# Causal mask of 128 tokens' scores: one 128-column matmul, or three rows of contraction and four triangles of 32

## The chip, the cores and the metric

The kernel runs on one core of a Trainium2 chip. The metric is the device time of one execution in microseconds. Engines: TensorE (PE: matmuls; PEld: its weight loads), VectorE (DVE), ScalarE (ACT), GpSimd (POOL) and SyncE (SP), which here only issues DMAs.

## The reference

Sixteen sequences of 256 tokens, 128 features wide, go through a mixture of experts, an attention with forget gates, and the same mixture again. What matters here is the attention:

```python
scores = jnp.einsum('bhid,bhjd->bhij', q, k) * scale       # 16 heads of 8
scores = scores + c[..., :, None] - c[..., None, :]         # c: cumulated log of the forget gates
causal = jnp.tril(jnp.ones((n, n), dtype=bool))
scores = jnp.where(causal, scores, NEG)                     # NEG = -1e30
attn = jax.nn.softmax(scores, axis=-1)
out = jnp.einsum('bhij,bhjd->bhid', attn, v)
```

## The kernel before

**Stages.** run_layers gives each engine its order of work: steps of the first mixture, then the attention, then the second mixture, with a few steps of two stages woven together at the borders. The attention goes through the 16 sequences as a pipeline; step s of it has six parts (j = 0 to 5), and in each part an engine does its share of sequence s (direct scores and their maxima), of s-1 (turned scores, exponentials, products with v), of s-2 (output projection) and of s+1, s+2 (projections to come). The steps in the middle are a loop of three unrolled steps (run_steps); the first two and the last three are written out. All engines run through their own list and meet at semaphores.

**Direct scores** (scores, called twice in each part, p = 0 to 11). They serve only for the row maxima of the softmax; the first starts at 111.2 us, the last mask at 364.3. For p = 0 to 3 (the first 128 tokens, t == 0) one matmul L881 takes four heads at once: q_dense (stationary, 104 rows of contraction) against k_heads (512 columns), into one of two PSUM banks. The 104 rows hold a split of q and k in three parts and the gates' sums, for four groups of heads; k_heads is zero outside a head's own group. For p = 4 to 11 (tokens 128 to 255) L886 does two heads in two matmuls of 256 columns. Then the mask: L889 adds ident16 (bfloat16, 128 x 128) times mask16 to the diagonal blocks of the bank, 4 x 128 columns for p < 4, 2 x 128 otherwise, and raises scores_ready. VectorE's row_max (L794) takes the negated maximum of the bank and raises max_done; scores p waits for the maximum of p-2, since the bank is the same.

**Turned scores** (L901, 12 a sequence, n = 0 to 11) are the transposed scores with the maxima as further rows of contraction, 512 columns each. The rows above the 106th are another form of the same mask: three rows later_q (-1e30 for queries ahead of token 32, 64, 96) against later_k (one for keys in the 32 tokens from there on) mask whole blocks of 32; what is left above the diagonal inside the blocks is cleared by GpSimd (L673) after the exponential. ScalarE takes the exponential of each (L733); L901 number n waits for exponential n-2. In part 0 ScalarE also copies turned maxima (L720, from the transpose L930) and issues two DMAs that put them into q_rows (L725), between exponentials 0 and 1.

**Products with v** (times_v, L916): for each of six pairs of exponentials, eight products of 32 stationary columns and 128 moving ones, each of which stands in the trace as two records (32 records in two calls). Their outputs go to partitions 32g to 32g+32 of a bank, g = 0 to 3 in turn.

**Order on TensorE in part 0**: scores 0, scores 1, turn_max (L930), L901 twice. **Part 1**: scores 2, scores 3, the projection of v (L960), L901 twice, L916 32 times.

**DMAs.** SP loads q_dense and k_heads for the next sequence from DRAM staging (L600, L603) once scores 3 of the current one are done (scores_ready). They fill rows 0 to 95 of q_dense (96 to 103 stay 1.0 from set_up_dense) and all 104 of k_heads. At the start constant_rows (L569) waits for the fills on GpSimd (dense_set, later_set) and sends constant rows to q_rows and k_rows by DMA (the issue of the last of them ends at 43.9 us); TensorE waits for all of them (ones_in, L940) ahead of the first score.

Of the kernel before, what the change touches and what calls it, by code (L numbers as in the profile page):

```python
# [5 lines left out]
FP32R = mybir.dt.float32r  # L6
# [6 lines left out]
P = 128  # L13
# [4 lines left out]
def at_least(eng, sem, value):  # L18

    if isinstance(value, int) and value <= 0:  # L20
        return
    eng.wait_ge(sem, value)
# [443 lines left out]
def attention_layer(nc, ctx, c, made, banks, x_all, S_LEN, before):  # L466
# [13 lines left out]
    H, D = c["H"], P  # L480
    NSEQ = x_all.shape[1] // 2
    HD = D // H
    NG, NU = 4, H // 4
    HW = 16
    ROWS = 3 * HD + 2
    KR = NG * ROWS
    KM = KR + 2
    KD = KM + 3
    SCALE = float(HD) ** -0.5
    N = S_LEN  # L490
    sb = lambda name, shape, dt: ctx.enter_context(nc.sbuf_tensor("a_" + name, shape, dt))
# [20 lines left out]
    k_parts = sb("k_parts", [P, 2, N], FP32R)  # L512
    q_rows = [sb(f"q_rows{b}", [KD, H, N], FP32R) for b in range(3)]
    k_rows = [sb(f"k_rows{b}", [KD, NU, N], FP32R) for b in range(3)]
    q_dense = sb("q_dense", [KR, NU, P], FP32R)
    k_heads = sb("k_heads", [KR, H, P], FP32R)
    v_sb = [sb(f"v{b}", [P, 2 * H // 2, 3, HW], FP32) for b in range(3)]
    neg_max = sb("neg_max", [P, 2, H], FP32)
    max_parts = sb("max_parts", [P, 2, 2, H], FP32R)
# [6 lines left out]
    ident16 = sb("ident16", [P, P], BF16)  # L526
    mask16 = sb("mask16", [P, 4, P], BF16)
    later_q = sb("later_q", [3, 2, P], FP32)
    later_k = sb("later_k", [3, 2, P], FP32)
# [8 lines left out]
    set_up, zeroed, ones_in, v_zeroed = sem("set_up"), sem("zeroed"), sem("ones_in"), sem("v_zeroed")  # L538
# [9 lines left out]
    scores_ready, max_done = sem("scores_ready"), sem("max_done")  # L548
# [12 lines left out]
    raw = lambda tile: tile[(slice(None),) * len(tile.shape)].bitcast(FP32)  # L561
# [7 lines left out]
    def constant_rows(sp):  # L569
        sp.wait_ge(zeroed, 4)  # L570
        ones = ones_r[:, :].bitcast(FP32).rearrange("r (u n) -> r u n", u=NU)
        for b in range(3):
            for g in range(NG):
                sp.dma_start(raw(q_rows[b])[NG * 3 * HD + g:KR:NG, NU * g:NU * (g + 1), :], ones).then_inc(ones_in, 16)
            sp.dma_start(raw(k_rows[b])[KR:KM, :, :], ones).then_inc(ones_in, 16)
        sp.wait_ge(dense_set, 2)
        sp.wait_ge(later_set, 5)
        for b in range(3):
            sp.dma_start(raw(q_rows[b])[KM:KD, :, :], later_q[:, :, :].rearrange("a t n -> a (t n)").unsqueeze(1)
                         .broadcast_to([3, H, N])).then_inc(ones_in, 16)  # L580
            sp.dma_start(raw(k_rows[b])[KM:KD, :, :], later_k[:, :, :].rearrange("a t n -> a (t n)").unsqueeze(1)
                         .broadcast_to([3, NU, N])).then_inc(ones_in, 16)
# [40 lines left out]
    def zero_rows(act, b):  # L623

        act.wait_ge(zero_set, 1)
        nc.scalar.activation(q_rows[b][:, :, :], zero_row[0:KD, :].unsqueeze(1).broadcast_to([KD, H, N]),
                             ACT.Copy).then_inc(zeroed, 1)
# [88 lines left out]
    def scalar(act):  # L716
# [23 lines left out]
        def part(i, s, j):  # L740
# [15 lines left out]
            if j == f_part(s) + 2 and F:  # L756
                act.wait_ge(qk_ready, n)
                at_least(act, q_stored, (n - 1) * 16 * 3)
                at_least(act, k_stored, (n - 1) * 16 * 3)
                nc.scalar.activation(q_parts[:, 0, :], q_ps, ACT.Copy, scale=SCALE)  # L760
                nc.scalar.activation(k_parts[:, 0, :], k_ps, ACT.Copy).then_inc(qk_hi_done, 1)
# [25 lines left out]
    def vector(dve):  # L787
# [39 lines left out]
        def part(i, s, j):  # L827
# [24 lines left out]
            if j == f_part(s) + 2 and F:  # L852
                dve.wait_ge(qk_hi_done, n)
                nc.vector.scalar_tensor_tensor(out=q_parts[:, 1, :], in0=q_ps, scalar=SCALE,
                                               in1=q_parts[:, 0, :].bitcast(FP32), op0=ALU.mult, op1=ALU.subtract).then_inc(qk_lo_done, 1)
# [18 lines left out]
    def tensor(pe):  # L874
        def scores(i, s, p):
            at_least(pe, max_done, i * 12 + p - 1)
            b, bank = s % 3, score_bank[p % 2]
            t, heads = (0, 4) if p < 4 else (1, 2)
            keys = (t + 1) * P
            if t == 0:  # L880
                nc.tensor.matmul(bank[:, :], q_dense[:, p, :], k_heads[:, p:H:NU, :], start=True, stop=False,  # L881
                                 skip_group_check=True)
            else:
                for n in range(heads):
                    h = 2 * (p - 4) + n
                    nc.tensor.matmul(bank[:, n * keys:(n + 1) * keys], q_rows[b][0:KR, h, P:N],  # L886
                                     k_rows[b][0:KR, h % NU, :], start=n == 0, stop=False, skip_group_check=True)
            own = bank[:, :].rearrange("p (h n) -> p h n", h=heads)[:, :, keys - P:keys]
            nc.tensor.matmul(own, ident16[:, :], mask16[:, 0:heads, :], start=False, stop=True,  # L889
                             skip_group_check=True).then_inc(scores_ready, 1)  # L890

        def turned_scores(i, s, n):
            if n == 0:
# [5 lines left out]
            t, u, jt = (0, n, 0) if n < 4 else (1, (n - 4) // 2, n % 2)  # L899
            rows = KD if jt == t else KM  # L900
            nc.tensor.matmul(bank[:, :], k_rows[b][0:rows, u, jt * P:(jt + 1) * P],  # L901
# [31 lines left out]
        def part(i, s, j):  # L933
# [3 lines left out]
                pe.wait_ge(w_ordered, 2)  # L937
            if s == 0 and j == 0:
                pe.wait_ge(set_up, 2)
                pe.wait_ge(ones_in, 16 * 3 * (NG + 3))  # L940
                pe.wait_ge(before["tiles_done"], 2 * NSEQ)
                pe.wait_ge(before["high_used"], 2 * NSEQ)

# [3 lines left out]
            if S:  # L947
                scores(i, s, 2 * j)
                scores(i, s, 2 * j + 1)
# [4 lines left out]
            if j == 1 and V:  # L954
# [4 lines left out]
                for t in range(2):  # L959
                    last = nc.tensor.matmul(side_bank[:, t * D:(t + 1) * D], xt[:, t * P:(t + 1) * P], c["Wv"][:, :],  # L960
                                            start=True, stop=True)
                last.then_inc(v_ready, 1)
            if j == 2 and F:
                at_least(pe, qk_lo_done, (n - 1) * 2)
                pe.wait_ge(xn_done, n)
                for t in range(2):
                    last = nc.tensor.transpose(proj_bank[:, t * P:(t + 1) * P], xn[:, t], c["ident"][:, :])
# [14 lines left out]
            if j == 4 and T:  # L982
# [7 lines left out]
                for t in range(2):  # L990
                    last = nc.tensor.transpose(side_bank[:, t * P:(t + 1) * P],
                                               attn[:, t].rearrange("p h d -> p (h d)"), c["ident"][:, :])
                last.then_inc(attn_t_ready, 1)
            if j == 5 and T:
                pe.wait_ge(attn_t_copied, i - 1)
                for t in range(2):
                    last = nc.tensor.matmul(side_bank[:, t * D:(t + 1) * D], attn_t[:, t * P:(t + 1) * P], c["Wo"][:, :],  # L997
                                            start=True, stop=True)
# [22 lines left out]
def program(nc, x, Wq, Wk, Wv, Wo, Wf, Wg, We, be, out):  # L1021
# [5 lines left out]
    with ExitStack() as ctx:  # L1027
# [17 lines left out]
        tiles = moe_tiles(nc, ctx, E, Q, D)  # L1045
        moe1 = moe_layer(nc, ctx, c, made, tiles, banks, x_all, "m1_", x_dram=x_rows)
        attention = attention_layer(nc, ctx, c, made, banks, x_all, N, before=moe1)
        moe2 = moe_layer(nc, ctx, c, made, tiles, banks[1:5] + [banks[0], banks[7]], x_all, "m2_",
                         out_dram=out_rows, before=attention)
# [72 lines left out]
```

## Time and profile before

| | us |
|---|---|
| runs, median of 3 | 467.35 (465.76 to 472.85) |
| the profiled execution's own time | 468.03 |
| its span, from first to last instruction | 465.9 |
| TensorE busy | 404.1 (87%) |
| VectorE busy | 362.4 (78%) |
| ScalarE busy | 278.5 (60%) |
| GpSimd busy | 249.7 (54%) |
| mean granted clock of TensorE | 0.978 |

All rows come from one profiled execution. Times of day are us from the start of its span. A record of a matmul begins when the instruction begins, which may be before its weights are loaded, and its end is modelled; so lengths are compared with each other and starts give the pace. "idle before <- X" tells how long the engine did nothing ahead of an instruction and who released it; "issue" means that no wait is seen. Some matmul records are missing.

### The profile page before, as it was taken

The page shows a single profiled execution, that of the slowest core. Times are in us where ns is not written, and L with a number is a line of the kernel's source. Part 1 is how long each engine was busy: PE and PEld are TensorE (multiplying, and loading weights), DVE is VectorE, ACT ScalarE, POOL GpSimd, SP SyncE. Part 2 cuts the span into 40 slices and gives each one's busy share as a digit, 9 for nine tenths or more (in the row PEclk, how much of TensorE's full clock was granted, in tenths as well). Part 3 has the DMA queues.
Part 4 walks back from the last instruction along what each step waited for, and adds up shares of the span by engine and source line. Part 5 has one row for each costly group of instructions (what it writes and reads, how often), then busy time and mean ns, then how long its engine had stood idle before and what let it go on. Part 6 is the DMA issues. An engine that isn't in the chain of part 4 may idle for free.

```text
span 465.9 us, 11688 instructions
## 1 busy us (share of the span) xinstructions
PE 404.1 (87%) x3280; PEld 287.6 (62%) x3296; DVE 362.4 (78%) x1284; ACT 278.5 (60%) x758; POOL 249.7 (54%) x431
## 2 busy tenths in 40 slices
PE   0778888775799999999999999999998898888884
PEld 0656666553466666666667666766765676666652
DVE  3989999986877786686677678677666458999995
ACT  4666777352275566657566566655656567667753
POOL 8976666543245544544554454454445435676654
PEclk9999999887999999999999999999999899999998
DMA  3311000035644354344535535443540000001001
GB/s 112 92 56 22 0 1 0 1 100 148 171 118 152 117 155 116 111 139 111 149 102 147 134 102 149 113 147 108 152 130 9 6 1 1 25 24 45 23 23 45
DMA packets 45792, 39.11 MB, mean 84 GB/s; under 512 B 5896, under 2 KB 42524, under 8 KB 45754
## 3 DMA queue, kind: packets, MB, share of 16 engines
q1 hardware_dynamic: 43706, 38.14, 29.0%
q10 hardware_dynamic: 2048, 0.53, 0.6%
q8 instruction: 17, 0.28, 0.3%
q14 instruction: 21, 0.17, 0.1%
HBM read 22.61 MB, written 15.20 MB: 81 GB/s over the span
## 4 chain that ended last, share of the span: by engine, by line
PE 43%; POOL 22%; issue 14%; ACT 8%; DVE 5%; DMA 2%; ACTq 2%; SPq 2%; POOLq 1%; DVEq 0%
PE bank L916 10%; POOL m_pair L217 9%; PE bank L901 8%; PE bank L886 6%; ACT a_weights L733 5%; POOL m_upper L221 4%; PE bank L889 4%; PE bank L881 4%; POOL m_rstd L229 3%; PE bank L997 2%; PE bank L1008 2%; ACTq L725 2%; PE bank L1011 2%; DVE a_neg_max L794 1%; DMA x_all<-in_L_attn_x 1%
## 5 line engine op out<-in xcount | busy, mean ns | idle before, releaser
L794 DVE TENSOR_REDUCE a_neg_max<-bank 128x2 f32<-128x512 f32 (+1 forms) x192 | 123.7, 685 | 62.6 <-PE bank L889 59.9
L673 POOL TENSOR_SCALAR_AFFINE_SELECT a_weights<-a_weights 128x512 f32<-128x512 f32 (+1 forms) x96 | 75.5, 787 | 108.7 <-ACT a_weights L733 104.0
L733 ACT ACTIVATE a_weights<-bank 128x512 f32<-128x512 f32 x192 | 107.0, 591 | 35.0 <-issue 22.0
L251 ACT ACTIVATE m_scaled<-bank,m_gates 128x128 f32<-128x128 f32 x256 | 72.3, 365 | 26.2 <-PE bank L417 26.2
L901 PE MATMUL bank<-a_q_rows,a_k_rows 106*128 106x512 f32 (+1 forms) x192 | 73.7, 451 | 4.9 <-ACT a_weights L733 4.9
L217 POOL TENSOR_TENSOR m_pair<-m_scaled 128x256 f32<-128x256 f32 x64 | 47.5, 742 | 50.8 <-ACT m_scaled L251 50.7
L294 DVE SCALAR_TENSOR_TENSOR m_lower<-bank,m_gates,m_lower 128x128 f32<-128x128 f32 x192 | 66.0, 344 | 2.3 <-issue 0.2
L886 PE MATMUL bank<-a_k_rows,a_q_rows 104*128 104x256 f32 x256 | 59.3, 335 | 0.4 <-DVE a_neg_max L794 0.4
L889 PE MATMUL bank<-a_mask,a_ident 128*128 128x256 bf16 (+1 forms) x176 | 56.2, 320 | 0.0
L916 PE MATMUL bank<-a_weights,a_v 128*32 128x128 f32 x1536 | 52.7, 279 | 0.0
L886 PEld LDWEIGHTS bank<-a_k_rows,a_q_rows 104*128 104x128 f32 x256 | 40.6, 194 | 14.5 <-DVE a_neg_max L794 10.1
L916 PEld LDWEIGHTS bank<-a_weights,a_v 128*32 128x32 f32 x1536 | 39.6, 111 | 8.9 <-issue 6.4
L416 PE MATMUL bank<-we_hi,m_xt_hi 128*128 128x512 f32 x64 | 32.1, 502 | 11.9 <-DVE m_lower L294 11.3
L901 PEld LDWEIGHTS bank<-a_q_rows,a_k_rows 106*128 106x128 f32 (+1 forms) x192 | 30.9, 193 | 13.4 <-ACT a_weights L733 11.4
L881 PE MATMUL bank<-a_k_heads,a_q_dense 104*128 104x512 f32 x64 | 31.1, 524 | 5.9 <-DMA a_k_heads<-k_stage 4.4
L720 ACT ACTIVATE a_max_t<-bank 32x128 fp32r<-32x128 f32 x32 | 8.5, 265 | 42.3 <-PE bank L930 42.3
L221 POOL TENSOR_TENSOR m_upper<-m_pair 128x128 f32<-128x128 f32 x64 | 29.6, 463 | 5.7 <-POOL m_pair L217 1.3
L889 PEld LDWEIGHTS bank<-a_mask,a_ident 128*128 128x128 bf16 x192 | 19.0, 99 | 19.4 <-issue 12.5
L275 ACT ACTIVATE m_xn<-x_all,m_shift,m_rstd 128x128 f32<-128x128 f32 (+1 forms) x64 | 26.3, 484 | 4.6 <-POOL m_shift L233 4.5
L416 PEld LDWEIGHTS bank<-we_hi,m_xt_hi 128*128 128x128 f32 x64 | 12.5, 196 | 22.6 <-DVE m_lower L294 22.1
L417 PE MATMUL bank<-we_hi,m_xt_hi 128*128 128x512 f32 x64 | 26.2, 409 | 0.0
L417 PE MATMUL bank<-we_lo,m_xt_hi 128*128 128x512 f32 x64 | 26.2, 409 | 0.0
(128 smaller groups left out, 828.5 us busy)
## 6 DMA issues: line engine op xcount, KB each, us to landing
a_k_rows<-k_stage SPq DMA_DIRECT2D x16, 416.0 KB
k_stage<-a_k_parts SPq DMA_DIRECT2D x48, 128.0 KB, 1.8
q_stage<-a_q_parts SPq DMA_DIRECT2D x48, 128.0 KB, 1.9
a_q_rows<-q_stage SPq DMA_DIRECT2D x64, 96.0 KB
a_k_heads<-k_stage SPq DMA_DIRECT2D x64, 52.0 KB
a_q_dense<-q_stage SPq DMA_DIRECT2D x16, 192.0 KB
x_all<-in_L_attn_x SPq DMA_DIRECT2D x8, 256.0 KB, 2.8
out_x<-x_all SPq DMA_DIRECT2D x8, 256.0 KB, 2.3
```

Of the source, the lines that this page charges most:

```text
L217: nc.gpsimd.tensor_tensor(pair[:, q % 2], scaled[:, q % 2, 0:2], scaled[:, q % 2, 2:4], ALU.add).then_inc(pair_done, 1)
L251: last = nc.scalar.activation(scaled[:, q % 2, j], y_high[q % 2][:, j * D:(j + 1) * D], ACT.Copy, scale=gates[:, s % 2, q, 4 + j:5 + j])
L294: nc.vector.scalar_tensor_tensor(out=lower[:, q % 2, j], in0=y_low[q % 2][:, j * D:(j + 1) * D], scalar=gates[:, s % 2, q, j:j + 1], in1=t ...
L417: last = nc.tensor.matmul(y_high[q % 2][:, :], x_part, w_part[:, H:2 * H], start=k == 0, stop=k == 2)
L673: nc.gpsimd.affine_select(out=diagonal, in_=diagonal, compare_op=ALU.is_ge, fill=0.0, base=0, pattern=[[0, heads.stop - heads.start], [1, P]],
L733: nc.scalar.activation(weights[n // 2][:, half:half + 4, :].rearrange("p h n -> p (h n)"), wt_bank[n % 2][:, :], ACT.Exp).then_inc(wt_exp, 1)
L794: nc.vector.tensor_reduce(neg_max[:, t, heads], score_bank[p % 2][:, :].rearrange("p (h n) -> p h n", n=(t + 1) * P), AX.X, ALU.max, negat ...
L881: nc.tensor.matmul(bank[:, :], q_dense[:, p, :], k_heads[:, p:H:NU, :], start=True, stop=False, skip_group_check=True)
L886: nc.tensor.matmul(bank[:, n * keys:(n + 1) * keys], q_rows[b][0:KR, h, P:N], k_rows[b][0:KR, h % NU, :], start=n == 0, stop=False, skip_g ...
L889: nc.tensor.matmul(own, ident16[:, :], mask16[:, 0:heads, :], start=False, stop=True, skip_group_check=True).then_inc(scores_ready, 1)
L901: nc.tensor.matmul(bank[:, :], k_rows[b][0:rows, u, jt * P:(jt + 1) * P], q_rows[b][0:rows, u:H:NU, t * P:(t + 1) * P], start=True, stop=T ...
L916: last = nc.tensor.matmul(out_bank[t][32 * g:32 * (g + 1), u // 2 * P:(u // 2 + 1) * P], v_sb[b][:, jt * H // 2 + 2 * g + u // 2, u % 2:u ...
```

## The change

For p < 4 the mask of whole blocks goes into L881 as three more rows of contraction (later_q and later_k, as L901 has them, set once at the start by two more DMAs), and only the triangles inside the four diagonal blocks of 32 are added by matmuls: four, one for each block of 32 queries, each with 32 stationary columns of ident16 and 4 x 32 moving columns of mask16, into 32 partitions. For p > 3 nothing changes.

```diff
--- before.py
+++ after.py
@@ -486,6 +486,7 @@
     KR = NG * ROWS
     KM = KR + 2
     KD = KM + 3
+    KL = KR + 3
     SCALE = float(HD) ** -0.5
     N = S_LEN
     sb = lambda name, shape, dt: ctx.enter_context(nc.sbuf_tensor("a_" + name, shape, dt))
@@ -512,8 +513,8 @@
     k_parts = sb("k_parts", [P, 2, N], FP32R)
     q_rows = [sb(f"q_rows{b}", [KD, H, N], FP32R) for b in range(3)]
     k_rows = [sb(f"k_rows{b}", [KD, NU, N], FP32R) for b in range(3)]
-    q_dense = sb("q_dense", [KR, NU, P], FP32R)
-    k_heads = sb("k_heads", [KR, H, P], FP32R)
+    q_dense = sb("q_dense", [KL, NU, P], FP32R)
+    k_heads = sb("k_heads", [KL, H, P], FP32R)
     v_sb = [sb(f"v{b}", [P, 2 * H // 2, 3, HW], FP32) for b in range(3)]
     neg_max = sb("neg_max", [P, 2, H], FP32)
     max_parts = sb("max_parts", [P, 2, 2, H], FP32R)
@@ -575,6 +576,8 @@
             sp.dma_start(raw(k_rows[b])[KR:KM, :, :], ones).then_inc(ones_in, 16)
         sp.wait_ge(dense_set, 2)
         sp.wait_ge(later_set, 5)
+        sp.dma_start(raw(q_dense)[KR:KL, :, :], later_q[:, 0:1, :].broadcast_to([3, NU, P])).then_inc(ones_in, 16)
+        sp.dma_start(raw(k_heads)[KR:KL, :, :], later_k[:, 0:1, :].broadcast_to([3, H, P])).then_inc(ones_in, 16)
         for b in range(3):
             sp.dma_start(raw(q_rows[b])[KM:KD, :, :], later_q[:, :, :].rearrange("a t n -> a (t n)").unsqueeze(1)
                          .broadcast_to([3, H, N])).then_inc(ones_in, 16)
@@ -886,8 +889,15 @@
                     nc.tensor.matmul(bank[:, n * keys:(n + 1) * keys], q_rows[b][0:KR, h, P:N],
                                      k_rows[b][0:KR, h % NU, :], start=n == 0, stop=False, skip_group_check=True)
             own = bank[:, :].rearrange("p (h n) -> p h n", h=heads)[:, :, keys - P:keys]
-            nc.tensor.matmul(own, ident16[:, :], mask16[:, 0:heads, :], start=False, stop=True,
-                             skip_group_check=True).then_inc(scores_ready, 1)
+            if t == 0:
+                for g in range(4):
+                    block = slice(32 * g, 32 * (g + 1))
+                    last = nc.tensor.matmul(own[block, :, block], ident16[:, block], mask16[:, 0:heads, block],
+                                            start=False, stop=True, skip_group_check=True)
+            else:
+                last = nc.tensor.matmul(own, ident16[:, :], mask16[:, 0:heads, :], start=False, stop=True,
+                                        skip_group_check=True)
+            last.then_inc(scores_ready, 1)
 
         def turned_scores(i, s, n):
             if n == 0:
@@ -937,7 +947,7 @@
                 pe.wait_ge(w_ordered, 2)
             if s == 0 and j == 0:
                 pe.wait_ge(set_up, 2)
-                pe.wait_ge(ones_in, 16 * 3 * (NG + 3))
+                pe.wait_ge(ones_in, 16 * (3 * (NG + 3) + 2))
                 pe.wait_ge(before["tiles_done"], 2 * NSEQ)
                 pe.wait_ge(before["high_used"], 2 * NSEQ)
 
```

## Rows read from the trace of the kernel before

**Rows 1.** The page: busy time by engine; the chain that ended last.

```profile
PE 404.1 (87%) x3280; PEld 287.6 (62%) x3296; DVE 362.4 (78%) x1284; ACT 278.5 (60%) x758; POOL 249.7 (54%) x431
...
PE 43%; POOL 22%; issue 14%; ACT 8%; DVE 5%; DMA 2%; ACTq 2%; SPq 2%; POOLq 1%; DVEq 0%
PE bank L916 10%; POOL m_pair L217 9%; PE bank L901 8%; PE bank L886 6%; ACT a_weights L733 5%; POOL m_upper L221 4%; PE bank L889 4%; PE bank L881 4%; POOL m_rstd L229 3%; PE bank L997 2%; PE bank L1008 2%; ACTq L725 2%; PE bank L1011 2%; DVE a_neg_max L794 1%; DMA x_all<-in_L_attn_x 1%
```

**Rows 2.** Stretches: us, busy us of PE, PEld, DVE, ACT, POOL, clock, DMA share.

```profile
108.00:156.88 48.88, 41.40 (x331) 27.56 (x334) 36.82 (x86) 23.03 (x56) 19.58 (x34) 0.93 0.48 137
223.08:239.52 16.44, 15.81 (x165) 11.07 (x165) 12.17 (x30) 10.19 (x24) 7.98 (x14) 1.00 0.47 127
288.92:304.99 16.07, 15.72 (x165) 11.02 (x165) 12.08 (x30) 10.07 (x24) 7.90 (x14) 1.00 0.48 130
```

**Rows 3.** Groups by shape of TensorE: count, busy us, mean ns of one.

```profile
L916 PE MATMUL bank<-a_weights,a_v 128*32 128x128 f32 x1536 | 52.7, 279 | 0.0
L889 PE MATMUL bank<-a_mask,a_ident 128*128 128x256 bf16 x128 | 36.7, 286 | 0.0
...
L889 PE MATMUL bank<-a_mask,a_ident 128*128 128x512 bf16 x48 | 19.6, 408 | 0.0
```

**Rows 4.** The chain through one loop sequence: start us, us, what.

```profile
224.84 0.56 ACT a_weights L733
225.43 0.61 ACTq L725
...
226.15 0.61 ACT a_weights L733
...
226.80 0.50 PE bank L901
```

**Rows 5.** Timeline of TensorE, same sequence: start us, us, operation.

```profile
223.40 0.59 PE L881 MATMUL bank<-a_k_heads,a_q_dense 104*128 104x512 f32 x1
223.83 0.39 PE L889 MATMUL bank<-a_mask,a_ident 128*128 128x512 bf16 x1
...
224.06 0.27 PE L930 MATMUL bank<-ident,a_max_parts 128*32 128x128 f32 x1
...
224.79 0.40 PE L881 MATMUL bank<-a_k_heads,a_q_dense 104*128 104x512 f32 x1
...
225.13 0.53 PE L881 MATMUL bank<-a_k_heads,a_q_dense 104*128 104x512 f32 x1
...
225.73 0.61 PE L960 MATMUL bank<-wv,a_xt 128*128 128x128 f32 x4
226.10 0.48 PE L901 MATMUL bank<-a_q_rows,a_k_rows 109*128 109x512 f32 x1
226.80 0.50 PE L901 MATMUL bank<-a_q_rows,a_k_rows 109*128 109x512 f32 x1 [0.22 <-ACT a_weights L733]
```

**Rows 6.** Into and out of L916, matmuls (PE) and weight loads (PEld).

```profile
222.68 0.40 PE L916 MATMUL bank<-a_weights,a_v 128*32 128x128 f32 x8
...
223.01 0.19 PEld L881 LDWEIGHTS bank<-a_k_heads,a_q_dense 104*128 104x128 f32 x1 [0.20 <-issue]
223.01 0.51 PE L881 MATMUL bank<-a_k_heads,a_q_dense 104*128 104x512 f32 x1
...
227.23 0.32 PE L916 MATMUL bank<-a_weights,a_v 128*32 128x128 f32 x4
...
228.24 0.30 PEld L886 LDWEIGHTS bank<-a_k_rows,a_q_rows 104*128 104x128 f32 x2 [0.20 <-issue]
```

**Rows 7.** The two L901 behind L960, in a sequence behind the loop.

```profile
307.97 0.96 PE L901 MATMUL bank<-a_q_rows,a_k_rows 109*128 109x512 f32 x2
```

**Rows 8.** First sequence: the weight load of p=2 and what it waited for.

```profile
113.21 0.29 PEld L881 LDWEIGHTS bank<-a_k_heads,a_q_dense 104*128 104x128 f32 x1 [0.41 <-DVE a_neg_max L794]
```

**Rows 9.** SP's queue at the end of the set-up and its next work.

```profile
41.28 1.83 SPq L579 DMA_DIRECT2D a_q_rows<-a_later_q  x1
...
96.58 1.32 SPq L609 DMA_DIRECT2D k_stage<-a_k_parts  x3
```

## The prediction

> **What bounds the kernel now.** I read the page's busy shares and its chain first [rows 1]: TensorE is busy for 87% of the span and carries 43% of the chain; the mask line L889 alone has 4% of the chain and L881, the product ahead of it, another 4%. Next the busy time in stretches [rows 2]. One sequence of the attention takes 16.44 us in the middle of the loop, and TensorE is busy for 15.81 us of it at a granted clock of 1.00; near the end a sequence takes 16.07 us. So the attention, from 111 to 364 us, is bound by TensorE, and time taken from or given to it there should show, unless another engine's wait lies over it. The groups by shape [rows 3] give the operation that is replaced: the 512-column mask lasts 408 ns by its record, against 286 ns for the 256-column one of the second half. The difference, 0.12 us for 256 columns, is what columns cost at the full clock: 0.06 us for 128. (The view has 48 records of the 64 wide masks that the loops give; some are missing.)
>
> The chain of one sequence [rows 4] then says which wait ends last. After the first turned score (L901), the chain goes to ScalarE: an exponential, the issue of a DMA (L725, 0.61 us), a second exponential, and back to L901 at 226.80. In that stretch TensorE isn't the bound, so what is done behind the first L901 and ahead of the one at 226.80 has cover. Scores p=0 and p=1 of a sequence stand ahead of that chain, p=2 and p=3 stand beside it.
>
> **How TensorE's time is read from its records** [rows 5]. A record of 512 columns lasts 0.39 to 0.40 us when its weight load was hidden; what is above that at its front is its load. So L881 for p=1 (starts 223.40, lasts 0.59) streams from 223.60; the one of p=0 streams from 223.13 (record 223.01, 0.12 of load ahead). Streams of p=0 and p=1 are 0.47 us apart; from p=1's to L930 (224.06) it is 0.46. For p=2 the stream begins at 224.80, p=3's at 225.27 (225.13 and 0.14), L960 at 225.73: 0.47 and 0.46 again. Of each 0.47, 0.23 is L881 and 0.24 is L889.
>
> **What the change adds in each of the four scores.** It takes out one load of 128 columns and one matmul of 512 columns and puts in four loads of 32 columns and four matmuls of 128 columns, whose outputs stand in four groups of 32 partitions. This form is in the kernel already: L916 has 32 stationary columns and 128 moving ones, and its outputs also go round the four groups. Its records in [rows 6]: two quads of four begin 0.11 us apart (eight records in flight last 0.40, one lasts 0.28), so the four groups do stream side by side. But it pays at both ends. Entering: the L901 ahead of it (226.80, 0.50 long, so 0.11 of load) has streamed by 227.12 to 227.14, and the first load of L916 starts at 227.23, though nothing else is late: 0.10 us of nothing. Its own first load stands in front, 0.02, and the four start 0.02 apart in all (four records take 0.32 against 0.30 for one). Leaving: the last quad streams until about 222.91, and the load of L881 starts at 223.01, 0.20 after the loader's last work: again 0.10 us of nothing, and then the 0.11 us of that load is in the open, where it is otherwise hidden under the matmul before. Between plain matmuls no such gap is seen: L889's record for p=1 starts at 223.83, where L881's 0.23 are over. L930, a transpose with 32 columns, starts right behind L889's 0.23 (224.06), so the width alone doesn't bring the gap; I take it that a transpose stays in the plain form.
>
> The Trainium skill, TensorEngine Tiling (Array Packing), Key Properties, says that a change of tiling mode, not of the tile alone, drains the engine; it has no figure. By that rule the new masks pay at both ends as L916 does, and the trace's 0.10 us is its price. The same page's Theoretical Speedup promises up to 4x for a dimension of 32 or less; by that alone the mask would go from 0.24 to about 0.06 us, which is the first rival below.
>
> So one score after the change, from L881's stream to the next stream: 0.23 (L881) + 0.10 (enter) + 0.02 (load) + 0.02 (four starts) + 0.06 (128 columns) + 0.10 (leave) + 0.11 (next load in the open) = 0.64.
> - p=0: 0.64 for 0.47, +0.17.
> - p=1: L930 follows, whose 32-column load costs some 0.03 in the open in place of 0.11: 0.56 for 0.46, +0.10.
> - p=2: +0.17. p=3: L960 follows, with a full load: 0.64 for 0.46, +0.18.
> The bounds of the unknown, that is of what bfloat16 quads behind a float32 product do: below, no gap at all (0.33, so -0.14 each); above, both gaps at L916's price. I take the upper one, as L916's rows are the nearest in form. Going below it would need the gap to belong to what L916 reads, and its gap on leaving is the same ahead of L881 and, at 228.24, ahead of L886 [rows 6].
>
> **What of it lies on the path.** p=0 and p=1 delay L901, and the ScalarE chain with it: +0.27 a sequence. p=2 and p=3 are +0.35 more, but TensorE waits for ScalarE afterwards: the L901 at 226.10 streams from 226.19 and is through at 226.42, the next one streams only from 226.91. That is 0.49 us of cover in a loop sequence, so the 0.35 is hidden; without this cover it would cost 0.35 x 15 = 5.3 us. In the three sequences behind the loop the two L901 last 0.96 together [rows 7], so the second streams from 308.54 where it could from 308.29: cover 0.25, and 0.10 us comes through. The first sequence has no turned scores beside it and runs at a lower clock; its p=2 waits 0.41 us for VectorE's maximum [rows 8], which partly covers a longer mask. Between 0 and 0.8 us, I take 0.4.
> Later stations of a sequence (row maxima, exponentials, the causal selects on GpSimd) follow TensorE and move with it. VectorE gets a mask's result no later for p=0: the last quarter starts about 0.37 us after L881's stream and lasts some 0.23 (L889's 0.286 less 0.06 for 128 columns), together 0.60, against 0.24 + 0.39 = 0.63 now. The three further rows of contraction in L881 cost nothing: L901 with 109 rows has the same record length, 0.50, as L881 with 104, 0.51 [rows 5, 6].
> Sum: 15 x 0.27 = 4.05; 3 x 0.10 = 0.30; 0.4; together 4.75 us.
>
> **Set-up.** Two more DMAs stand in SP's queue ahead of the six of L579 and L581, of which the longest issue takes 1.83 us [rows 9]. So up to 3.7 us, and the last would be issued by 47.6 in place of 43.9; SP has nothing more until 96.58. The cover is some 49 us; without it the attention would start 3.7 us later. TensorE's wait at the first score asks for two more DMAs on the same semaphore, which have landed long before 111 us. The two fills on GpSimd get three more partitions and no more elements in each.
>
> **The sum against the time.** The profiled execution took 468.03 us (span 465.9 and 2.1 around it), so it would become 472.8. It was 0.68 above the median of the runs, 467.35; the forecast for the median is 472.1.
>
> **Rivals.**
> - *The quads stream beside everything without a gap.* Then p=0 takes 0.23 + 0.02 + 0.02 + 0.06 = 0.33 for 0.47, the same for p=1 unless the issue of L930 and L901 holds them back; p=2 and p=3 only lengthen the wait for ScalarE. 15 x 0.14 to 15 x 0.28 is 2.1 to 4.2 us less: 465.2 to 463.1. It decides where a gap plus open load costs less than 0.14 together. For it: the quads of L916 do overlap. Against: the gaps around L916, at each of its groups that I looked at. Chance 0.12. The skill's page TensorE: Matmul & The Clock Gate, Measured speedup vs the span model, has a pack of tiles last one matmul and some 4 ns a tile, which says the same of the inside and nothing of the ends.
> - *The cover over p=2 and p=3 is gone,* because ScalarE's DMA issue or exponentials come sooner and TensorE is again the last. Then 0.62 x 15 + 0.4 = 9.7 us: 477.1. For it: the sequences behind the loop have only half the cover. Against: 0.61 us of DMA issue stands in every loop sequence. Chance 0.10.
> - *Nothing shows,* because the longer masks fall into waits for VectorE's maxima, as in rows 8, or the gap is smaller next to a bfloat16 quad: 467 to 469. For it: the L881 of p=3 already has 0.14 us of its load in the open (0.53 for 0.39) [rows 5]. Chance 0.12.
> - *The clock.* Eight more gaps in a sequence lower TensorE's activity, and the granted clock, 1.00 in the middle [rows 2], falls in stretches. The attention's first 48.88 us had 0.93; a mean of 0.93 is 14% of the time at half speed (1.2 GHz in place of 2.4), which loses up to 7% of 250 us, 17 us, and with half of it under other waits still 8 us over the forecast: 480 and up. Chance 0.04.
>
> **The numbers.** Forecast 0.62, with its own range of 469.5 to 474.5: 472.1 us. For 8 in 10 the range reaches to where the first and second rival begin: 465.0 to 477.1. A change of 2% (9.3 us) is about what a measurement can tell: faster than 458.0 lies beyond the first rival's end, 0.01; slower than 476.7 is most of the second and the fourth, 0.10; within, 0.89.
>
> **What the profile after would show.** Right: a gap of about 0.10 us ahead of the first 32-column mask load and behind the last quarter, L881 records of about 0.50 (load in the open) for p=1 and p=3; streams of p=0 and p=1 0.64 apart; the idle time of the L901 at the ScalarE wait shorter by some 0.35; the sequence in the loop at about 16.7 us in place of 16.44. Wrong: the L881 of p=1 starting 0.33 behind p=0's (first rival), or a sequence of 17.1 us with no wait for ScalarE left (second), or granted clocks under 1.00 between 130 and 350 us (fourth).

## The result and the profile after

The change made the kernel slower: 474.78 us median of 4 runs (473.20 to 476.32) against 467.29 for the kernel before (465.76 to 472.85), a ratio of 1.0157 with a 95% interval of 1.0109 to 1.0205. That is 7.5 us by the medians, where 4.75 were forecast. (The ratios here and below are those of the record, which aren't the quotients of the medians; for some of the kernels the two differ by 0.4%.) The profiled execution took 476.32 us, its span is 474.3.

The page of the kernel after: busy time, granted clock in 40 slices of 11.9 us, and the chain. They answer to [rows 1].

```profile
PE 413.4 (87%) x3488; PEld 292.6 (62%) x3488; DVE 362.8 (76%) x1284; ACT 278.5 (59%) x758; POOL 249.5 (53%) x431
...
PEclk9999999995579999899999999999999979999999
...
PE 47%; POOL 21%; issue 14%; ACT 6%; DVE 5%; DMA 2%; SPq 2%; ACTq 1%; POOLq 1%; DVEq 0%
```

The mean granted clock fell from 0.978 to 0.960; slices 10 and 11 show 5 tenths, and slice 12 shows 7, where the first two sequences of the attention run. In the trace the clock is low (0.50) from 108.4 to 135.7 us. The busy time in stretches (us, busy us of PE, PEld, DVE, ACT, POOL, clock, DMA share), first after, answering to [rows 2]: the first two sequences, one with a dip of the clock, one in the loop, one behind it.

```profile
109.72:126.60 16.88, 14.83 (x57) 9.15 (x58) 10.84 (x24) 2.85 (x9) 2.67 (x5) 0.50 0.45 122
126.60:144.01 17.41, 17.38 (x136) 11.52 (x137) 11.45 (x26) 9.53 (x22) 7.42 (x12) 0.74 0.45 125
193.76:212.34 18.58, 17.52 (x181) 11.98 (x177) 12.98 (x32) 10.13 (x24) 8.73 (x15) 0.91 0.44 125
245.31:261.81 16.50, 16.07 (x181) 11.12 (x177) 12.08 (x30) 10.12 (x24) 7.98 (x13) 1.00 0.44 126
294.78:311.06 16.28, 15.93 (x181) 11.10 (x177) 12.04 (x30) 10.06 (x24) 7.90 (x13) 1.00 0.44 128
```

The first two of before, cut at the same places, that is from one sequence's first score to the next:

```profile
111.18:125.27 14.09, 11.34 (x44) 7.21 (x46) 10.72 (x24) 2.65 (x8) 2.67 (x5) 0.77 0.53 147
125.27:139.96 14.69, 13.71 (x124) 9.21 (x125) 11.24 (x26) 9.38 (x22) 7.41 (x12) 1.00 0.53 148
```

Here is the time. The first two sequences take 34.29 us in place of 28.78, +5.51, at a clock of 0.50 and 0.74 for 0.77 and 1.00. The one with the dip takes 18.58 against 16.61 for its counterpart, +1.97; the clock was low there for 3.4 us. The other loop sequences don't get longer: the first of them takes 16.75 for 16.86, the seven others have a mean of 16.49 us, and the eight of before one of 16.51. The three sequences behind the loop take 16.28, 16.25 and 16.24 for 16.07, 16.08 and 16.64, and the one after them, up to the last sequence's first score, 14.62 for 14.02. The rest of the span's 8.4 us is a start of the attention 1.46 us earlier and an end (from the last sequence's first score on) 1.88 us longer, both in stages that the change doesn't touch. The clock was at its lower level there too: ahead of the attention for twice 3.4 us in the profile of before and not at all in this one, and in the second mixture for 3.4 us before and 6.8 us after.

The groups by shape, answering to [rows 3]:

```profile
L884 PE MATMUL bank<-a_k_heads,a_q_dense 107*128 107x512 f32 x64 | 32.9, 514 | 5.3 <-DMA a_k_heads<-k_stage 4.1 <-DVE a_neg_max L797 1.0 <-issue 0.2
...
L895 PE MATMUL bank<-a_mask,a_ident 128*32 128x128 bf16 x256 | 15.8, 238 | 0.0
```

And TensorE in a loop sequence, with VectorE's addition L874 (L871 of before) beside it, answering to [rows 5, 6]:

```profile
244.97 0.40 PE L926 MATMUL bank<-a_weights,a_v 128*32 128x128 f32 x8
...
245.30 0.19 PEld L884 LDWEIGHTS bank<-a_k_heads,a_q_dense 107*128 107x128 f32 x1 [0.20 <-issue]
...
245.67 0.41 DVE L874 TENSOR_TENSOR x_all<-x_all,bank 128x256 f32 x1
245.72 0.10 PEld L895 LDWEIGHTS bank<-a_mask,a_ident 128*32 128x32 bf16 x4 [0.24 <-issue]
245.73 0.24 PE L895 MATMUL bank<-a_mask,a_ident 128*32 128x128 bf16 x4
...
245.89 0.19 PEld L884 LDWEIGHTS bank<-a_k_heads,a_q_dense 107*128 107x128 f32 x1
...
246.32 0.24 PE L895 MATMUL bank<-a_mask,a_ident 128*32 128x128 bf16 x4
246.49 0.10 PEld L940 LDWEIGHTS bank<-ident,a_max_parts 128*32 128x32 f32 x1
...
246.53 0.30 PEld L911 LDWEIGHTS bank<-a_q_rows,a_k_rows 109*128 109x128 f32 x2
...
249.16 0.19 PEld L911 LDWEIGHTS bank<-a_q_rows,a_k_rows 109*128 109x128 f32 x1 [0.34 <-ACT a_weights L736]
```

The last of these rows is the load of the sequence's fourth turned score, which waits for ScalarE. The same load in the kernel before, for the sequence that starts at 239.45:

```profile
243.27 0.19 PEld L901 LDWEIGHTS bank<-a_q_rows,a_k_rows 109*128 109x128 f32 x1 [0.57 <-ACT a_weights L733]
```

The four small masks stand as one row: they start together at 245.73 and last 0.24 in all. The first load of theirs starts 0.42 behind L884's, of which 0.11 is L884's own load and 0.21 its columns: 0.10 of nothing, as forecast. The next L884 load starts 0.17 behind the masks, again with 0.10 of nothing, and lies in the open (that matmul's record lasts 0.49). From score to score it is 0.59 us, where before it was 0.47.

### The profile page after: what moved, and what is told of

The parts are those of the page before. It is cut to its first block, busy times and chain, and to the rows that moved or that the text cites. A ratio compares the mean times of both kernels' runs of the same rounds, so it can differ in the third digit from the quotient of the medians.

```text
span 474.3 us, 12090 instructions
## 1 busy us (share of the span) xinstructions
PE 413.4 (87%) x3488; PEld 292.6 (62%) x3488; DVE 362.8 (76%) x1284; ACT 278.5 (59%) x758; POOL 249.5 (53%) x431
## 4 chain that ended last, share of the span: by engine, by line
PE 47%; POOL 21%; issue 14%; ACT 6%; DVE 5%; DMA 2%; SPq 2%; ACTq 1%; POOLq 1%; DVEq 0%
PE bank L926 10%; POOL m_pair L217 9%; PE bank L911 8%; PE bank L889 6%; PE bank L884 5%; POOL m_upper L221 4%; ACT a_weights L736 3%; POOL m_rstd L229 3%; PE bank L898 3%; PE bank L970 2%; PE bank L895 2%; PE bank L1007 2%; PE bank L1018 2%; PE bank L1021 2%; DMA x_all<-in_L_attn_x 1%
## 5 line engine op out<-in xcount | busy, mean ns | idle before, releaser
L911 PE MATMUL bank<-a_q_rows,a_k_rows 106*128 106x512 f32 (+1 forms) x192 | 74.7, 462 | 2.3 <-ACT a_weights L736 2.3
L889 PE MATMUL bank<-a_k_rows,a_q_rows 104*128 104x256 f32 x256 | 61.5, 345 | 0.1
L889 PEld LDWEIGHTS bank<-a_k_rows,a_q_rows 104*128 104x128 f32 x256 | 42.6, 203 | 14.7 <-DVE a_neg_max L797 9.1
L416 PE MATMUL bank<-we_hi,m_xt_hi 128*128 128x512 f32 x64 | 31.4, 491 | 13.9 <-DVE m_lower L294 13.2
L898 PE MATMUL bank<-a_mask,a_ident 128*128 128x256 bf16 x128 | 37.9, 296 | 0.0
L884 PE MATMUL bank<-a_k_heads,a_q_dense 107*128 107x512 f32 x64 | 32.9, 514 | 5.3 <-DMA a_k_heads<-k_stage 4.1
L911 PEld LDWEIGHTS bank<-a_q_rows,a_k_rows 106*128 106x128 f32 (+1 forms) x192 | 32.0, 202 | 8.1 <-ACT a_weights L736 7.1
L417 PE MATMUL bank<-we_hi,m_xt_hi 128*128 128x512 f32 x64 | 25.6, 400 | 0.0
L417 PE MATMUL bank<-we_lo,m_xt_hi 128*128 128x512 f32 x64 | 25.6, 399 | 0.0
L416 PE MATMUL bank<-we_lo,m_xt_hi 128*128 128x512 f32 x64 | 25.5, 399 | 0.0
```

The lines of the kernel that those rows point to most:

```text
L416: nc.tensor.matmul(y_low[q % 2][:, :], x_part, w_part[:, 0:H], start=k == 0, stop=k == 2)
L898: last = nc.tensor.matmul(own, ident16[:, :], mask16[:, 0:heads, :], start=False, stop=True, skip_group_check=True)
```

## The experiments

All ratios are against runs of the kernel before on the same chip; its medians there were 467.89 (the first four kernels), 466.93 (the next four) and 468.15 us (the last four). The stretches come from one profile of each kernel. "Sequence" is from one sequence's first score to the next one's.

**Rows and set-up without the small masks.** The changed kernel keeps the wide mask.

```diff
-            if t == 0:
+            if t == 0 and False:
                 for g in range(4):
```

> The changed kernel with its two set-up DMAs and the 107 rows of contraction, but the one wide mask matmul of before (its -1e30 adds to that of the coarse rows; nothing is left out). Clock theory (the four small masks make the first two sequences too light for TensorE to get its clock back): 467 us, as before, low clock for about 7 us at the attention's start, first two sequences 14.1 and 14.7 us. Rival (set-up DMAs or rows cost it): 474 us.

468.98 us, ratio 1.0007 (0.9964 to 1.0050). First two sequences 13.85 and 15.46 us, low clock for 6.8 and 3.4 us, loop 16.44 to 16.63. The two DMAs and the three rows cost nothing that can be measured, within 0.4 to 0.5% (some 2 us) either way; what costs is the small masks.

**Small masks from the third sequence on, and in the first two alone** (there the condition is s < 2).

```diff
-            if t == 0:
+            if t == 0 and s >= 2:
```

> The four small masks only from the third sequence on; the first two keep the wide mask beside the coarse rows. Clock theory: the first two sequences take 14.1 and 14.7 us again, and the whole 467 to 470 us (2 us more for each stretch of low clock later in the loop). Rival (the masks themselves cost it, 0.27 us in each sequence as forecast): 471 us, with 14.1 and 14.7 us first and 16.8 us in the loop.

> The reverse: the small masks in the first two sequences only. Clock theory: 472 to 474 us, with 16.9 and 17.4 us for the first two sequences at a granted clock near 0.5. Rival (cost in each sequence): 468 us.

From the third on: 470.24 us, ratio 1.0021 (0.9986 to 1.0057). First two alone: 473.14 us, ratio 1.0073 (1.0035 to 1.0112). Their stretches, the late one first (two sequences), then the early one (two sequences and one in the loop):

```profile
111.28:124.84 13.56, 10.67 (x45) 6.68 (x46) 10.87 (x24) 2.74 (x9) 2.67 (x5) 0.82 0.55 152
124.84:140.23 15.39, 14.96 (x125) 10.15 (x125) 11.23 (x26) 9.32 (x22) 7.37 (x12) 0.89 0.51 142
```

```profile
111.41:128.20 16.79, 14.55 (x57) 9.10 (x57) 10.85 (x24) 2.66 (x8) 2.69 (x5) 0.54 0.44 123
128.20:145.18 16.98, 16.53 (x136) 11.07 (x136) 11.42 (x26) 9.51 (x22) 7.42 (x12) 0.80 0.48 129
228.10:244.60 16.50, 15.85 (x176) 11.12 (x168) 12.23 (x30) 10.19 (x24) 8.05 (x14) 1.00 0.47 128
```

So most of the loss comes with the small masks of two sequences out of sixteen, and the other fourteen give little: 470.24 against 468.98 for the kernel with the rows alone. The two intervals overlap a little; the stretches are clear, 33.77 us against 28.95 for the first two sequences. The 16.7 to 16.8 us that the forecast and the rival above wanted in the loop aren't there (16.45 to 16.54 in the late one). Within the early kernel's ten runs the time goes with the granted clock: two runs with 0.977 took 468.28 and 468.62 us, six with 0.958 to 0.962 took 473.08 to 475.18, one with 0.967 took 471.93; a tenth with 0.929 took 470.21 and doesn't fit. So the same kernel is some 5 us shorter in the runs with the higher clock.

**Filling TensorE's idle time ahead of the first score.** 16 matmuls whose result is overwritten.

```diff
+            if s == 0 and j == 0:
+                for n_fill in range(16):
+                    nc.tensor.matmul(score_bank[0][:, :], ident16[:, :], mask16[:, :, :], start=True, stop=True)
             if j == 0 and S:
                 pe.wait_ge(rows_in, (i + 1) * 16 * LOADS)
```

> The changed kernel with 16 matmuls of 512 columns, whose result is overwritten, put into TensorE's idle time of 4 us ahead of the first score. Clock theory: the clock no longer falls there, the first two sequences go to 14 and 14.5 us or less, and the time to 466 to 469 us. Rival (the longer first sequences are the masks' own): 474 us, first two sequences 16.9 and 17.4 us as before the filling.

470.53 us, ratio 1.0050 (1.0009 to 1.0090); first two sequences 16.18 and 16.60 us. Better than 474.8, but neither expectation was met: the clock still fell, only later, at 114.0 us for 10.2 us and at 127.6 for 6.8. Matmuls ahead of the scores aren't enough. So the next pair adds some in the first sequence as well.

**Filling the first sequence too,** in the changed kernel and in the kernel before, beside the 16 matmuls ahead of it:

```diff
             if S:
                 scores(i, s, 2 * j)
                 scores(i, s, 2 * j + 1)
+            if s == 0:
+                for n_fill in range(4):
+                    nc.tensor.matmul(wt_bank[0][:, :], ident16[:, :], mask16[:, :, :], start=True, stop=True)
```

> The changed kernel with 16 discarded matmuls ahead of the first score and 4 more in each of the six parts of the first sequence, so that TensorE is hardly idle there. Clock theory: granted clock 1.00 through the first two sequences, which then take 13 to 15 us each with the small masks too, and 466 to 469 us in all, equal within 1 us to the wide mask with the same filling. Rival (the masks themselves cost 0.27 us a sequence): 4 us more than the wide mask with the same filling.

> The kernel before with the same filling. Clock theory: 465 to 467 us, first two sequences about as quads_kept. Rival (each sequence costs): 464 to 466 us, and quads_kept 4 us above it. It would also be the version that beats both, if the low clock at the start of the attention costs the kernel before anything.

Changed kernel 468.52 us, ratio 1.0040 (0.9998 to 1.0082); kernel before 465.73 us, ratio 0.9966 (0.9930 to 1.0002). Their first two sequences, the changed kernel's first:

```profile
110.41:126.28 15.87, 13.62 (x83) 7.80 (x81) 11.47 (x26) 3.08 (x10) 2.83 (x6) 1.00 0.49 143
126.28:140.59 14.31, 13.79 (x136) 9.26 (x136) 11.09 (x25) 9.35 (x22) 7.49 (x13) 1.00 0.53 150
```

```profile
109.40:124.09 14.69, 13.26 (x70) 7.70 (x69) 10.44 (x24) 2.81 (x9) 2.68 (x5) 1.00 0.51 142
124.09:138.79 14.70, 13.84 (x124) 9.21 (x124) 11.70 (x27) 9.42 (x22) 7.65 (x13) 1.00 0.54 156
```

The clock is 1.00 in all four stretches, and the two sequences take 30.18 and 29.39 us: the 5.5 us between the kernels have become 0.8. With the clock held the whole difference is 2.8 us in place of 7.5 by the medians, 0.74% in place of 1.57% by the ratios. I had expected 1 or 4, and it lies between: the price in a sequence isn't 0.27, and it isn't nothing.

**No triangles at all** in the first 128 tokens' scores (`first` is the product L884, which now ends the group):

```diff
-                for g in range(4):
-                    block = slice(32 * g, 32 * (g + 1))
-                    last = nc.tensor.matmul(own[block, :, block], ident16[:, block], mask16[:, 0:heads, block],
-                                            start=False, stop=True, skip_group_check=True)
+                last = first
```

> The changed kernel without the triangle masks (left out: the row maxima of the first 128 tokens then run over later keys in the same block of 32). Both ends of the mask go, 0.38 us a score. Theory of cover (TensorE's own issue of instructions and the wait for ScalarE hide the small masks in the loop): the loop sequence goes from 16.5 to 16.1-16.4 us. Rival (p=0 and p=1 are on the path in full): 15.7 us.

468.50 us, ratio 1.0016 (0.9977 to 1.0055). A miss for both theories: the loop sequences take 16.43 to 16.58 us at full clock, as with either mask. (The median says less, since the clock moved here too: the ten runs have means of 0.957 to 0.978.) Without these masks TensorE has four matmuls less in each of the four scores and the loop is no faster, so TensorE's work in the scores isn't what the loop waits for. The timeline of this kernel shows which wait ends last there:

```profile
238.85 0.30 PEld L884 LDWEIGHTS bank<-a_k_heads,a_q_dense 107*128 107x128 f32 x2 [0.20 <-issue]
...
239.21 0.41 DVE L874 TENSOR_TENSOR x_all<-x_all,bank 128x256 f32 x1
...
239.86 0.28 PE L937 MATMUL bank<-ident,a_max_parts 128*32 128x128 f32 x1 [0.28 <-DVE x_all L874]
240.08 0.30 PEld L908 LDWEIGHTS bank<-a_q_rows,a_k_rows 109*128 109x128 f32 x2
```

L937 (L930 of before, the transpose of the maxima) has a named wait here: 0.28 us for VectorE's addition of the projection into x_all. Both use side_bank; the transpose may write it only when VectorE has read it (proj_added). In the other kernels this wait is taken by TensorE's sequencer ahead of L930, while matmuls that were issued earlier still run, so no idle time of TensorE is recorded for it. It stands in the trace as a semaphore instruction on the load queue, before and after:

```profile
L22 PEldq EVENT_SEMAPHORE  x1: 51/51/51, 240.3 to 240.3; - x1
L22 PEldq EVENT_SEMAPHORE  x1: 51/51/51, 246.1 to 246.1; - x1
```

It begins 0.04 us behind the addition's end in all three kernels, and the load of the first turned score begins 0.41 behind it. Against the first load of the sequence the addition ends at the same place in all three, 0.77 to 0.78 us (before 240.22 behind 239.45, after 246.08 behind 245.30, here 239.62 behind 238.85), and so does the load of the first turned score: 1.22, 1.23 and 1.23 us.

This kernel also shows something of the clock. It gives TensorE less to do in the first two sequences than the small masks do, yet in its profile the clock was low for twice 6.8 us (first two sequences 13.76 and 16.60 us) and not for 27.3. That profile is of one of its two runs with the highest clock, and the low stretches of the others aren't known.

**Each group of small masks twice, with one plain matmul between.**

```diff
+                for again in range(2):
                     for g in range(4):
                         ...
+                    if again == 0:
+                        nc.tensor.matmul(own[:, 0:1, 0:32], ident16[:, :], mask16[:, 0:1, 0:32], start=False,
+                                         stop=False, skip_group_check=True)
```

> The changed kernel with the four small masks twice, and one plain matmul of 32 columns between the two groups (the masked places get -2e30 or -3e30; nothing is left out), which adds one leaving and one entering and a load: some 0.4 us a score. If a switch costs what L916 shows, L884 to L884 goes from 0.59 to about 1.0 us. Theory of cover: p=0 and p=1 add 0.8 less what is left of cover, the whole sequence 17.2 to 17.5 us, 486 to 492 us in all. Rival (all hidden): 16.5 us and 475 us.

486.57 us, ratio 1.0382 (1.0314 to 1.0451), loop sequences 17.36 to 17.43.

```profile
269.65 0.49 PE L884 MATMUL bank<-a_k_heads,a_q_dense 107*128 107x512 f32 x1
270.08 0.24 PE L896 MATMUL bank<-a_mask,a_ident 128*32 128x128 bf16 x4
270.25 0.19 PE L899 MATMUL bank<-a_mask,a_ident 128*128 128x32 bf16 x1
270.37 0.24 PE L896 MATMUL bank<-a_mask,a_ident 128*32 128x128 bf16 x4
270.54 0.49 PE L884 MATMUL bank<-a_k_heads,a_q_dense 107*128 107x512 f32 x1
```

From score to score it is now 0.89 us (269.65 to 270.54) in place of 0.59. The added pair of switches with its two short pieces of work costs 0.30, less than the 0.4 expected: the plain matmul starts 0.17 behind the small ones and they 0.12 behind it, so a switch with little streaming around it is still the 0.10 of nothing, but the bfloat16 load isn't in the open. Four scores get 1.2 us more work, and the sequence grows by 0.87; once TensorE's part of the sequence is long enough it is the bound again. Here too the clock was low at the start, for 17.1 and 10.2 us, although TensorE has more to do than with the small masks once.

**VectorE's addition earlier,** with the wide and the small masks, and both once more with the filling:

```diff
-            if j == 5 and X:
-                normalise(i - 1, s - 1, 0)
             if j == 5 and T:
                 ...
                 nc.vector.tensor_tensor(pair, pair, side_bank[:, 0:2 * D], ALU.add).then_inc(proj_added, 1)
+            if j == 5 and X:
+                normalise(i - 1, s - 1, 0)
```

> The kernel before with VectorE's addition of the projection into x_all moved ahead of the normalising of the next output (two instructions, some 0.46 us). Theory: in the loop TensorE's first transpose L930 and all behind it wait for that addition to free the bank it reads, and not for TensorE's own work; then the loop sequence goes from 16.5 to 16.1-16.3 us and the time to 464 us. Rival (TensorE's own work is what bounds the loop): 16.5 us and 467 us, as before.

> The same move in the changed kernel. Theory: with VectorE out of the way the small masks are what ends last, so the loop sequence stays at 16.4 to 16.5 us, 0.2 above the wide mask with the same move, and the time at 472 to 475 us. Rival (something else bounds both): both kernels have the same loop sequence.

> The kernel before with both: the discarded matmuls that keep TensorE's clock up at the start of the attention, and the early addition. If both theories hold they add: 462 to 464 us, the fastest of all, clock 0.99 or more.

> The changed kernel with both. Theory: 466 to 468 us, that is 3 to 4 us above the wide mask with both, 0.2 us in each sequence now that neither VectorE nor the clock stands before it. Rival (no cost of its own in a sequence): equal to the wide mask with both within 1 us.

Wide mask: 466.07 us, ratio 0.9967 (0.9935 to 0.9999). Small masks: 472.90 us, ratio 1.0059 (1.0015 to 1.0103). With the filling too: wide 466.78 us, 0.9956 (0.9925 to 0.9988); small 468.27 us, 1.0002 (0.9963 to 1.0042). Seven loop sequences in one row, wide masks first, small ones second:

```profile
172.06:285.98 113.92, 110.57 (x1145) 76.97 (x1148) 85.03 (x204) 70.95 (x168) 55.94 (x92) 1.00 0.46 128
```

```profile
177.74:292.95 115.21, 112.35 (x1236) 77.60 (x1232) 84.85 (x204) 70.87 (x168) 56.04 (x92) 1.00 0.46 127
```

That is 16.27 us a sequence with the wide mask and 16.46 with the small ones. The timeline says why, the addition, the first load and the load of the first turned score, wide masks and then small ones:

```profile
237.04 0.38 DVE L869 TENSOR_TENSOR x_all<-x_all,bank 128x256 f32 x1
...
237.14 0.19 PEld L881 LDWEIGHTS bank<-a_k_heads,a_q_dense 104*128 104x128 f32 x1 [0.20 <-issue]
...
238.19 0.30 PEld L901 LDWEIGHTS bank<-a_q_rows,a_k_rows 109*128 109x128 f32 x2
```

```profile
243.47 0.38 DVE L872 TENSOR_TENSOR x_all<-x_all,bank 128x256 f32 x1
...
243.57 0.19 PEld L884 LDWEIGHTS bank<-a_k_heads,a_q_dense 107*128 107x128 f32 x1 [0.20 <-issue]
...
244.77 0.32 PEld L911 LDWEIGHTS bank<-a_q_rows,a_k_rows 109*128 109x128 f32 x2
```

The addition now ends 0.28 to 0.29 us behind the first load. The wide-mask kernel uses it: its first turned score comes 1.05 us behind the first load in place of 1.22. The small-mask kernel can't: 1.20. So here the small masks show their price, 0.15 us on the path of each sequence, 0.19 us in the mean sequence. In the sequences behind the loop, where TensorE passes the wait for the addition early, the same two figures stand in the profiles of before and after, without any move: 1.05 and 1.20.

Three kernels with the wide mask are 0.3 to 0.4% below the kernel before, at the edge of what the runs can tell: the filling alone (0.9966, its interval ends at 1.0002), the early addition alone (0.9967, up to 0.9999) and both together (0.9956, up to 0.9988). Together they were to be 462 to 464 us and are 466.78, where the early addition alone is 466.07 on the same chip; that the two add up isn't shown, and the expectation of 462 to 464 was a miss. So was the one for small masks with both: 1.5 us above the wide mask, where 3 to 4 were expected. Without the filling the same pair lies 6.8 us apart, so the filling takes most of the difference away here as well.

## Why the prediction was right or wrong

The direction was right, and 474.78 us lies within 465.0 to 477.1, though just outside the 469.5 to 474.5 that the forecast itself was given. The account of where the time goes was wrong in its largest terms: 4.05 of the 4.75 us were to come at 0.27 a sequence and hardly any of that came in the loop, and the first sequences, put at 0.4 for one of them, gave 5.5. That the time came out in the range is luck, two errors of opposite sign.

- **The two gaps: right.** "0.10 us of nothing" on entering and on leaving, and the next load in the open, are in the timeline of the kernel after. The sum for a score was 0.64 and measured 0.59: L884 streams for 0.21 and not 0.23, the four start within 0.01 and not 0.02, and their first load isn't in the open.
- **"TensorE is busy for 15.81 us of it ... So the attention ... is bound by TensorE": the step that failed.** A record of a matmul is some 0.17 us longer than its streaming (0.39 for 0.21 to 0.23), and records that follow each other overlap and leave no idle time between them; 96% busy doesn't say that the next matmul couldn't have been later. For L930 and the first L901 I took TensorE's own work as the last to end. The runs show VectorE's addition: no_triangles has the same 16.5 us with no mask matmul in these scores, and the early addition gives 16.27. The term 15 x 0.27 = 4.05 was about 0 in the loop, and 0.2 in each of the sequences behind it.
- **"p=1: +0.10".** Here the order in TensorE's sequencer hid it. Before, the waits and additions on registers ahead of L930 and L901 came behind the mask's start, and L901's load 0.42 us behind it. After, they run while TensorE sits in the gap, and L911's load stands 0.04 behind L940's. With no room left in VectorE's chain (the early-addition pair) the price of p=0 and p=1 together is 0.15 and not 0.27.
- **"p=2 and p=3 are hidden": right.** The load of the fourth turned score still waits for ScalarE, 0.34 us in place of 0.57; the wait was to get shorter by 0.35 and did by 0.23. Behind the loop 0.10 was to come through above the 0.27; measured is 0.2 in all (16.07 to 16.28), of which 0.15 is the later load of the first turned score (1.05 to 1.20).
- **The set-up at nothing: right** (rows_only).
- **The fourth rival, given 0.04, is the main cause.** I looked for a falling clock in the middle, where TensorE has work enough, and put its price at 8 us and more. Its main fall was at the start of the attention, where the clock was low already: [rows 2] shows 0.93 there, and I took 0.4 us for the whole first sequence. The sign that the prediction named for this rival, a clock under 1.00 between 130 and 350 us, is there (to 135.7, and 3.4 us from 197.1). With wide masks the clock is low for 6.8 us in the profile of before, and for 6.8 and once more 3.4 in those of rows_only, quads_late and before_early_add; with small ones for 27.3 us (after), or for 17.1 and 6.8 (quads_early, quads_early_add). Small masks alone in two sequences bring most of the loss, and discarded matmuls in the same place take it back. Together: of 7.5 us, some 4.7 go with the filling (7.5 less 2.8; by the ratios 3.9). The remaining 2.8 have, by the two profiles, 0.8 in the first two sequences and 0.2 in each of those written out behind the loop, 0.4 in the last. Another 1.0 there is a later start of the attention, ahead of any mask.
- **What stays open.** Why the clock stays low with the small masks isn't shown. That they leave TensorE too little to do was the theory of the experiments, and the filling bears it out. Against it, no_triangles has still less to do and its profile had 13.7 us of low clock, and two_switches has more and had 27.3. The rival is that the gaps, or the small matmuls themselves, do it; no run separates the two. The one dip in the loop (16.6 to 18.6 us) was in one of the profiles only; whether small masks make such dips more likely wasn't settled. Single sequences of 17.0 to 17.3 us at full clock also occur with wide masks (one in before_kept). And two parts of the span vary between kernels that are equal or nearly so there. The end (from the last sequence's first score) goes with the clock in the second mixture: 113.0 to 113.2 us where it didn't fall before the last 4 us of the span, 113.9 to 114.8 with 3.4 us of low clock, 115.8 to 116.1 with 6.8, 116.7 and 116.8 with 10.2 (two_switches left out). The first score comes at 109.2 to 109.9 us where the clock hadn't fallen before the idle time ahead of it, and at 110.4 to 111.4 where it had. One profile of each kernel can't tell whether masks have a part in these falls.

## What to carry to other kernels

A group of small matmuls in column groups, put between plain ones, cost here 0.20 us of gaps and 0.11 us of open load, more than its shorter columns saved. Weigh that before a wide matmul is split; whether such groups are cheaper beside others of their kind wasn't tried. Before a cost on an engine is put on the path, look for the waits its sequencer takes between matmuls: remove the work altogether in one run, and if the period doesn't move, find the semaphore that ends last. And look at the granted clock by stage before a stage is put down at a fraction of a microsecond: here a change of 0.12 us a score came with a clock that stayed low in a stage where it was low already, and its two sequences got 5.5 us longer.

## What the runs showed of the hardware

TensorE's clock stayed at its lower level (1.2 of 2.4 GHz) through a first sequence in which its records fill 14.83 of 16.88 us; with the small masks the four masks of that sequence stream 128 columns each (four groups side by side) in place of 512. With 24 wide matmuls added in the sequence and 16 ahead of it the clock was 1.00 throughout, and the records fill 13.62 of 15.87 us. So the busy time of the records alone doesn't tell at which level the clock is.

The Trainium skill, TensorEngine Tiling (Array Packing), Key Properties, has the drain at a change of tiling mode; the trace agrees, with 0.10 us on each side and in both data types. Four bfloat16 matmuls in four column groups start within 0.01 us; the skill's TensorE: Matmul & The Clock Gate gives about 25 ns from start to start as the least (Wait — 56ns, not 53.3ns?), which these starts in different groups are well under; the some 4 ns a tile that the prediction has from the skill's same page (Measured speedup vs the span model) is near them.
